# DLRM tower on one Trainium2 core: row-by-row reads on the sync engine, relative ids and a new order on ScalarE

## What is computed

```
e = stack([tbl_f[ids[:, f]] for f in range(27)], axis=1)     # 2048 x 27 x 128
z = einsum('bnd,bmd->bnm', e, e)[pairs i < j]                # 351 per sample
h = maximum(concat([z, dense_ctx]) @ W_top1 + b_top1, 0)     # 367 -> 512
h = maximum(h @ W_top2 + b_top2, 0)                          # 512 -> 256
y = h @ W_top3                                               # 256 -> 1
```

## Time and profile before

| | |
|---|---|
| median of three runs | 383.83 us (383.69 to 386.02) |
| the profiled execution, by itself | 381.17 us |
| its span in the trace | 379.3 us |
| mean granted clock of TensorE | 0.987 |

### The profile page before, as it was taken

The page is one execution under the profiler, slowest core; times in us unless marked ns, Lnnn a source line. Parts: engine busy times, 40 slices in busy tenths (PEclk is TensorE's granted clock), DMA queues, the critical chain, the costliest instruction groups (busy, mean ns, idle before and its releaser), DMA issues.

```text
span 379.3 us, 9954 instructions
## 1 busy us (share of the span) xinstructions
PE 345.7 (91%) x4035; PEld 322.6 (85%) x4035; DVE 294.4 (78%) x821; ACT 153.3 (40%) x217; POOL 269.3 (71%) x287
## 2 busy tenths in 40 slices
PE   1788868599999999999999999999999999999985
PEld 1677767588999999998999999998999999998874
DVE  4986696898688969798689969798689869793432
ACT  3352644434343453534343453534243453533421
POOL 6777877777777777777777777777777777777400
PEclk9989996999999999999999999999999999999999
DMA  6995225953333333334333333333343343221100
GB/s 184 251 247 136 64 63 137 213 186 96 82 93 85 79 84 82 95 69 95 82 94 85 79 86 81 95 72 91 85 91 85 76 89 83 76 57 50 36 2 1
DMA packets 22988, 36.38 MB, mean 96 GB/s; under 512 B 6224, under 2 KB 17120, under 8 KB 22944
## 3 DMA queue, kind: packets, MB, share of 16 engines
q0 software_dynamic: 8896, 18.24, 20.2%
q1 hardware_dynamic: 14048, 17.52, 18.6%
HBM read 35.73 MB, written 0.01 MB: 94 GB/s over the span
## 4 chain that ended last, share of the span: by engine, by line
PE 75%; POOL 14%; issue 5%; DMA 3%; ACT 2%; DVE 1%; ACTq 0%; DVEq 0%
PE embT_ps L410 35%; PE gram_ps L442 13%; POOL emb L379 12%; PE h_ps L470 11%; PE h_ps L494 7%; PE embT_ps L420 6%; DMA emb<-in_tbl,idx 3%; PE flat_ps L453 2%; POOL flatT L379 2%; ACT embT L634 1%; DVE flat L568 1%; DMA idx<-in_idx_rows 0%; PE h_ps L481 0%; PE flat_ps L481 0%; DVE flat L569 0%
## 5 line engine op out<-in xcount | busy, mean ns | idle before, releaser
L379 POOL DMA_INDIRECT emb<-in_tbl,idx x272 | 261.8, 962 | 83.8 <-issue 80.6
L537 DVE TENSOR_SCALAR one_hot<-ids,row_of 125x256 fp32r<-125x256 int32 x658 | 205.4, 383 | 13.2 <-PE embT_ps L410 10.6
L410 PE MATMUL embT_ps<-one_hot,tbl 125*128 125x256 f32 x1284 | 182.0, 297 | 13.0 <-DVE one_hot L537 11.4
L410 PEld LDWEIGHTS embT_ps<-one_hot,tbl 125*128 125x128 f32 x1284 | 166.7, 196 | 17.9 <-issue 8.9
L634 ACT COPY embT<-embT_ps 128x256 f32<-128x256 f32 x77 | 48.0, 624 | 134.2 <-PE embT_ps L410 129.0
L642 ACT COPY embT<-embT_ps 128x512 f32<-128x512 f32 (+1 forms) x80 | 80.7, 1012 | 11.7 <-PE embT_ps L420 11.7
L568 DVE STREAM_TRANSPOSE flat<-gram_ps 128x864 f32<-128x864 f32 x31 | 33.5, 1082 | 43.7 <-PE gram_ps L442 43.1
L442 PEld LDWEIGHTS gram_ps<-embT 128*59 128x59 f32 x1984 | 56.2, 134 | 9.6 <-ACT embT L634 3.9
L442 PE MATMUL gram_ps<-embT 128*59 128x54 f32 x1984 | 60.2, 217 | 3.8 <-ACT embT L634 2.3
L420 PE MATMUL embT_ps<-ident,emb 128*128 128x128 f32 x272 | 43.8, 276 | 11.6 <-DMA emb<-in_tbl,idx 8.6
L420 PEld LDWEIGHTS embT_ps<-ident,emb 128*128 128x128 f32 x272 | 32.2, 142 | 13.8 <-DMA emb<-in_tbl,idx 11.4
(11 more groups left out here) (47 smaller groups left out, 85.0 us busy)
## 6 DMA issues: line engine op xcount, KB each, us to landing
ids<-in_ids_hot SPq DMA_DIRECT2D x77, 128.0 KB
emb<-in_tbl,idx POOLq DMA_INDIRECT x272, 3.1
embT<-in_tbl SPq DMA_DIRECT2D x5, 448.0 KB
w_sb<-in_tbl SPq DMA_DIRECT2D x3, 560.0 KB
w_sb<-in_W_ring SPq DMA_DIRECT2D x1, 756.0 KB
w_sb<-in_W_top SPq DMA_DIRECT2D x1, 512.0 KB
h1T<-in_tbl SPq DMA_DIRECT2D x1, 448.0 KB
w_sb<-in_tbl SPq DMA_DIRECT2D x1, 448.0 KB
```

The lines of the kernel that those rows point to most:

```text
L379: pool.indirect_dma_start(gathered_row(t, s), None, tables[f][:, :], bass.IndirectOffsetOnAxis(ap=idx[:, t, f:f + 1], axis=0),).then_inc(g ...
L410: mm = pe.matmul(out[:, 0:HN], tbl[0:ROWS, part, AT[o] + chunk, :], one_hot[0:ROWS, k % SLOTS, c, :], start=(chunk == 0 and part == 0), st ...
L537: done = dve.tensor_scalar(one_hot[0:ROWS, k % SLOTS, c, :], of, row_of[0:ROWS, KINDS.index(CH[o]), chunk:chunk + 1], None, ALU.is_equal)
```

## The change

It has three parts.

1. *Row reads on the sync engine.* In tiles 9 and 15 the last gathered feature (s = 16, quad 4) is no longer gathered by GpSimd. The sync engine reads its 128 rows one by one into a new buffer `one_by_one`: in a stretch of 16 it loads 16 ids into registers and issues 16 DMAs of one row. A tile is eight stretches, and `due(n)` puts one behind every third load of ids: those of tile 9 behind loads 34, 37, ..., 55, those of tile 15 behind 56, 59, ..., 77. Quad (9, 4) and quad (15, 4) wait for all 128 rows.
2. *Relative ids on ScalarE.* For the first 17 hots ScalarE replaces the ids in their buffer by the float `row - id` (an activation with scale -1 and the row number as bias); VectorE then compares with the constant `-chunk` in place of an int32 compare against `row_of`.
3. *ScalarE's order.* The high part of the table to come is written after a hot is copied, not ahead of it, and then the relative ids of hot n + 2.

With that, the ids of the gathers are laid out by the new feature order, and those of the three more features of tiles 0 and 1 come in a load of their own (`idx_more`). `row_i` and `place` now lie in `h2`.

```diff
+BY_ROW = (9, 15)
+STRETCH = 16
...
+    STRETCHES = TILE // STRETCH
+    APART = 3
+
+    def due(n):
+        done = []
+        for i, t in enumerate(BY_ROW):
+            last = min(len(HOT0) + O * (t + 1) // HT - 2, len(HOTS))
+            done += [i * STRETCHES + m for m in range(STRETCHES) if last - APART * (STRETCHES - 1 - m) == n]
+        return done
...
+            def read_rows(m):
+
+                n, r = divmod(m * STRETCH, TILE)
+                t = BY_ROW[n]
...
+                sp.load(row_ids, ids_hot[O:O + 1, t * TILE + r:t * TILE + r + STRETCH])
+                for i in range(STRETCH):
+                    row = sp.snap(row_ids[i], min_val=0, max_val=tables[f_row].shape[0] - 1)
+                    sp.dma_start(one_by_one[r + i:r + i + 1, n % 2, :],
+                                 tables[f_row][bass.ds(row, 1), :]).then_inc(row_landed[n % 2], 16)
...
             for n in range(EARLY, len(HOTS)):
                 load_ids(n)
...
+                for m in due(n):
+                    read_rows(m)
+            for m in due(len(HOTS)):
+                read_rows(m)
...
             def turn(t, q):
-                pe.wait_ge(gathered[t % EB][q], 16 * rows_landed(t, q))
+                if gathers(t, q):
+                    pe.wait_ge(gathered[t % EB][q], 16 * rows_landed(t, q))
+                if len(gathers(t, q)) < len(quad(t, q)):
+                    pe.wait_ge(row_landed[BY_ROW.index(t) % 2], 16 * TILE * (BY_ROW.index(t) // 2 + 1))
...
-                dve.wait_ge(ids_loaded[n % IDS], 16 * (n // IDS + 1))
+                if n < RELATIVE:
+                    dve.wait_ge(ids_relative, n + 1)
+                else:
+                    dve.wait_ge(ids_loaded[n % IDS], 16 * (n // IDS + 1))
...
+                        if n < RELATIVE:
+                            done = dve.tensor_scalar(columns, of.bitcast(F32), float(-chunk), None, ALU.is_equal)
...
+            def relative_ids(n):
+
+                act.wait_ge(ids_loaded[n % IDS], 16 * (n // IDS + 1))
+                if n == 0:
+                    act.wait_ge(rows_ready, len(KINDS))
+                kind = KINDS.index(CH[HOTS[n][2]])
+                act.activation(ids[0:ROWS, n % IDS, :].bitcast(F32), ids[0:ROWS, n % IDS, :], ACT.Identity,
+                               bias=row_of[0:ROWS, kind, 0:1], scale=-1.0).then_inc(ids_relative, 1)
...
             AHEAD = 3
+            LEAD = 2
             for o in range(AHEAD):
                 split_high(o)
+                relative_ids(o)
             for kind, *of in ORDER:
                 if kind == "hot":
                     n = READ["hot", of[0], of[1]]
-                    if n + AHEAD < WHOLE:
-                        split_high(n + AHEAD)
-                    elif n in SPLIT_AT:
-                        split_high(SPLIT_AT[n])
...
                     copy_hot(*of)
+
+                    if AHEAD <= n + LEAD < WHOLE:
+                        split_high(n + LEAD)
+                    elif n + 1 in SPLIT_AT:
+                        split_high(SPLIT_AT[n + 1])
+                    if AHEAD <= n + LEAD < RELATIVE:
+                        relative_ids(n + LEAD)
```

More of the change, by code:

```diff
@@ L116, in quad, with gathers @@
         return range(q * QUAD, min(FEATS - len(hots_of(t // HT)), (q + 1) * QUAD))
+    def gathers(t, q):
+        return [s for s in quad(t, q) if not (t in BY_ROW and s == GF - 1)]
     def rows_landed(t, q):
-        return sum(len(quad(s, q)) for s in range(t % EB, t + 1, EB))
+        return sum(len(gathers(s, q)) for s in range(t % EB, t + 1, EB))
     def plan(t):
@@ L209, in dlrm_tower @@
         h2 = sb("h2", [P, H2])
+        row_i = h2[:, 0:len(KINDS) * max(CH)].bitcast(I32).rearrange("p (k c) -> p k c", k=len(KINDS))
+        place = h2[:, H2 - 1:H2].bitcast(I32)
         y_sb = sb("y_sb", [P, T])
@@ L215, in dlrm_tower @@
         ident = sb("ident", [P, P])
-        place = sb("place", [P, 1], I32)
+        one_by_one = sb("one_by_one", [P, 2, D])
         second = sb("second", [P, 1], I32)
@@ L227, in gathered_row @@
         def gathered_row(t, s):
+            if t in BY_ROW and s == GF - 1:
+                return one_by_one[:, BY_ROW.index(t) % 2, :]
             if s >= GF:
@@ L230, in gathered_row, with id_of @@
             return emb[:, t % EB, s, :]
+        def id_of(t, s):
+            return idx[:, t, s:s + 1] if s < GF else idx_more[:, t, s - GF:s - GF + 1]
         def raw(o, a, b):
@@ L287, in dlrm_tower @@
         gathered = [[sem(f"gathered{b}_{q}") for q in range(QUADS)] for b in range(EB)]
+        row_landed = [sem(f"row_landed{b}") for b in range(2)]
         turned = sem("turned")
@@ L328, in load_table @@
                     sp.dma_start(raw(o, a, b), rows[a:b, :]).then_inc(staged[o], 16)
-            sp.dma_start(idx[:, 0, :], idx_rows[:, 0, :]).then_inc(idx_first, 16)
+            row_ids = [sp.alloc_register(f"row_id{i}") for i in range(STRETCH)]
+            f_row = by_row_feature(FEATS)
+            def read_rows(m):
+                n, r = divmod(m * STRETCH, TILE)
+                t = BY_ROW[n]
+                if n > 1 and r == 0:
+                    sp.wait_ge(turned, TURNED["quad", BY_ROW[n - 2], QUADS - 1])
+                sp.load(row_ids, ids_hot[O:O + 1, t * TILE + r:t * TILE + r + STRETCH])
[3 more added lines that the diff above has]
+                                 tables[f_row][bass.ds(row, 1), :]).then_inc(row_landed[n % 2], 16)
+            sp.dma_start(idx[:, 0, :], idx_rows[:, 0, 0:GF]).then_inc(idx_first, 16)
             for o in range(SHARED + 1):
@@ L374, in _ @@
                 for q in range(QUADS):
-                    if t >= EB:
+                    if t >= EB and gathers(t, q):
                         pool.wait_ge(turned, TURNED["quad", t - EB, q])
-                    for s in quad(t, q):
+                    for s in gathers(t, q):
                         f = GATHERED[s]
+                        if t == 0 and s == GF:
+                            pool.wait_ge(idx_further, 16)
                         pool.indirect_dma_start(
                             gathered_row(t, s), None, tables[f][:, :],
-                            bass.IndirectOffsetOnAxis(ap=idx[:, t, f:f + 1], axis=0),
+                            bass.IndirectOffsetOnAxis(ap=id_of(t, s), axis=0),
                         ).then_inc(gathered[t % EB][q], 16)
```

23 lines of the change are left out of this document (15 added, 8 removed).

## The result

The changed kernel takes **408.37 us** (median of 6 runs, 406.21 to 409.13) against 383.27 us for the kernel before (6 runs, 382.17 to 386.02): the ratio is 1.067 with a 95% interval of 1.0635 to 1.0706. The forecast was slower, 399.5 us with a range of 393 to 415. Sign, place and mechanism came true; the size was 9 us short.

What follows compares the result with a forecast made beforehand. GpSimd's gathers were taken to bound the kernel before 82 us, TensorE after. Stall 13.2 + clock 2.0 + front 0.5 = 15.7 us, on a median of 383.83 us gave 399.5 us, range 393 to 415.

Steps and rivals of the forecast that it cites:

- the main case: One stall in tile 9, with a stretch between 6.4 and 11.3 us: 393.5 to 404 us by itself, chance 0.58.
- What bounds the kernel: Before 82 us only what moves a gather moves the end; after it every wait put on TensorE is paid in full.
- The place and kind of the stall: At quad (9, 4) TensorE waits for tile 9's last 16 rows, queued behind load 55, which is let go at 235.57.
- Its size, 13.2 us: TensorE's wait at quad (9, 4), from 234.80 until the last row lands at 247.97: 13.2 us, 8.4 at least.
- S: Time of one stretch on the sync engine: 7.0 rows + 1.6 register steps + 2.0 register loads = 10.6 us (5.8 to 16.2).
- A backlog of 0 while S < 11.3: Stretches behind every third load of ids fit into the sync queue's 12.5 us per three loads: cost 0.
- The sync engine paces the kernel: Rival: stretches over 11.3 us make the sync queue set the pace; 419 us at 12.8 us each, chance 0.24.
- The clock, 2 us: After the stall at quad (9, 4) TensorE's granted clock drops to half for a while: 2 us (0 to 4).
- Tile 15's row reads free: Tile 15's last stretch follows the last load of ids at 323.2, 20 us ahead of need even 16 us later: cost 0.
- The rest of tile 9's row reads at nothing: Row reads other than the last stretch make loads of ids up to 6 us late, within the buffers: cost 0.
- The front, +0.5: Before 82 us, new timing of GpSimd's gathers costs 1.0 us less 0.5 from VectorE's faster compare: +0.5 (-5 to +5).
- the shut-out rival: VectorE's new float compare blocks GpSimd's gathers, mostly before 82 us: some 6 us, 405.5 us, chance 0.13.

Runs made afterwards that it cites:

- order only: Changed kernel without row reads, relative ids and float compare, so ScalarE's new order alone: 382.24 us, ratio 1.0002 to the kernel before.
- earlier rows: Two kernels with tile 9's row reads six loads of ids earlier: the changed kernel otherwise, 388.43 us; also without relative ids and float compare, 384.63 us.
- one register load: Changed kernel with the sync engine's id registers loaded only ahead of the first stretch: 395.65 us, ratio 1.0342 to the kernel before.
- no rows: Changed kernel with no row reads, both features gathered as before: 384.59 us, ratio 1.0058 to the kernel before.
- earlier: Changed kernel with tile 9's stretches six loads of ids earlier, the last behind load 49: 388.43 us, ratio 1.0183 to the kernel before.

## Why the prediction was right, point by point

The kernel is slower and the forecast mechanism is there, but 408.4 us lies above what the main case was given by itself, 393.5 to 404. It lies in the range because the range had room for longer stretches; the sum did not lead there.

- **What bounds the kernel, and that a stall is paid in full.** Right. The 19.4 us at quad (9, 4) are still there at the end: +23.1 at that quad, +25.1 at tile 15.
- **The place and kind of the stall.** Right: the last stretch stands behind load 55, which is let go only after TensorE needs the rows. Moving tile 9's stretches, with nothing else changed, took it away.
- **Its size, 13.2 us for 19.4.** This is the step that failed. Of S = 10.6, the rows with their register step were put at 8.6 and took 7.0: a row is 0.41 to 0.44 us in all, since its DMA takes 0.23 and not the 0.36 of the sync engine's plain issues, and the step fits into the rest. The two register loads were put at 2.0, "nearer to the transfers", and took 6.4 with their gaps; the shortest of each in the profile, 1.01 and 1.67 us, are together already above 2.0, and the bound of 2.8 was no bound. The Trainium skill, "Runtime: NRT & Kernel Launch", has some 200 ns per register in its section on instruction fetch (not in the one that the prediction names), for which I had worked out an estimated 3.6 us; the trace has 2.7 us at best and 6.1 here.
- **A backlog of 0 while S < 11.3.** The idea was right, its input wrong, and the threshold a mean over loads that aren't let go evenly. The two stretches that count, those ahead of load 55, took 12.2 and 12.9 us, where 10.6 each was what loads 49 to 55 left room for (23.8 us, less some 1.3 for the loads at each). That gives the 4.0 us; at the forecast S of 10.6 it would have been about 0. The last stretch, 13.3 us (243.53 to 256.87), stands behind load 55 and has no part in it. The kernel with four loads between stretches shows the price.
- **The sync engine paces the kernel** (the rival at 0.24) came half true: S passed the threshold, but VectorE never waits for a load of ids in the changed kernel; its only waits for ids are 2.6 us in all, for ScalarE's relative ones in the front. Loads that are 4 us late lie within the three hots of the buffers, as worked out; so the time is 408 and not 419.
- **The clock, 2 us.** 2.4 us, right. The 1.6 us in the last 10 us of the span weren't in it, and they aren't the stall's: without row reads the same 12 products took 2.77 us, with stretches four loads apart 2.84, where the kernel before, order only and the kernels with earlier rows show 1.60. What sets off this lower clock was not found.

```profile
373.57 2.77 PE L543 MATMUL h_ps<-flatT,w_sb 126*128 126x128 f32 x12 [0.57 <-ACT flatT L732]
```

- **Tile 15's row reads free.** Right; the shift is the same ahead of them and behind.
- **The rest of tile 9's row reads at nothing.** Wrong by 2.7 us in the profile and some 2.5 in the runs: a late gather beside them was not in the sum. I had followed whom the queue delays, not what its work does to the transfers of others.
- **The front, +0.5 with VectorE's compare as a rival.** In the one profile it is +0.6, a near hit by luck: by quad (9, 4) the same front has cost 1.9, 2.3 and 5.3 us in the profiles of one register load, no rows, and earlier. VectorE did get faster, and nobody needed it. These are its groups after (operation and tile, form, count, busy us, mean ns), where the old form had 383 ns in the kernel before:

```profile
L606 DVE TENSOR_SCALAR one_hot<-ids,row_of 125x256 fp32r<-125x256 int32 x516 | 159.5, 381 | 28.9 <-PE embT_ps L469 28.9
...
L604 DVE TENSOR_SCALAR one_hot<-ids 125x256 fp32r<-125x256 f32 x142 | 33.6, 301 | 6.4 <-ACT ids L699 2.6
```

  The order costs nothing measurable and the relative ids with their compare 1.3 to 2.2 us, mostly through GpSimd: the direction of the shut-out rival at about a third of its 6 us. The Trainium skill's "SBUF — State Buffer", in "Who interferes with whom", lets the two engines block each other fully in such a mode. No run shows in which mode the compare was; a gather beside it loses 0.08 us (1.02 and 1.03 for 0.94).

The sum with measured terms is 19.6 (stall) + 2.4 (clock) + 2.7 (late gather) + 0.6 + 0.2 - 0.4 (front and drift) + 1.6 (clock at the end) = 26.7 us, the difference of the two profiles; forecast were 15.7.

## What to carry to other kernels

An issue queue that serves two masters must be costed with everything that stands in it: of one stretch, the register loads, which no list of transfers shows, were half the time, and they counted twice, once in the last stretch and once as backlog. When no row prices an operation that goes to memory and back, don't put it below the nearest transfer; ask what the sum does at three times the value. Before moving work to an idle engine, look for the one item whose release comes after its use: here the same reads, six places earlier in the queue, cost 0.7% in place of some 6%.

## What was not expected of the hardware

- A load of registers from memory on the sync engine takes between 1.0 and 4.2 us for the tensor's address and between 1.7 and 3.7 us for 16 ids, in one execution. In the changed kernel the gap for both was 3.0 us after three loads of ids spread over 7.12 us (280.16 to 283.20), and 6.3 and 6.4 behind loads bunched into 1.31; but 4.3 behind another such bunch (291.53 to 295.81), so the bunch alone doesn't set it.
- A row DMA whose address is in a register issues in 0.23 us, and 16 with their register steps go out in 6.6 to 7.0 us.
- The late gather at quad (8, 2) came at a DMA share of only 0.3 to 0.5 of the 16 engines (the changed kernel, 200 to 206 us by the microsecond). Two kernels show it at the same place beside slow register loads. The share didn't tell of this delay.
- With the relative ids VectorE's compare got faster and the kernel slower: 0.08 us less for each of 142 instructions, and some 2 us more until the 56th gather.
